# A two-layer latent-attention kernel on one core: a new order for the first tile of the first cross-attention, and a values product in halves in the second

## Chip, core and metric

The kernel runs on one core of a Trainium2 chip. The time is the device time of one execution in microseconds (us); the time of a version is the median over several runs. The engines are TensorE (PE), with its weight loads shown apart as PEld, VectorE (DVE), ScalarE (ACT), GpSimd (POOL) and SyncE (SP, which issues the DMAs). Each has its own instruction stream and works it off in order; they meet in semaphores.

## What is computed

`x` is 16 × 64 × 256 in float32, the context 16 × 256 × 256. Six stages follow one another, each as a residual on a layer norm of `x`:

```python
x = x + L0_xattn(layernorm(x), ctx)      # 16 heads of 64, own layer norms of both, scores clipped to +-11
x = x + L0_attn(layernorm(x))            # latent attention with rotary part, causal
x = x + L0_ffn(layernorm(x))             # attention, then 8 experts, top 2
x = x + L1_xattn(layernorm(x), ctx)      # 16 heads of 16, key padding mask
x = x + L1_attn(layernorm(x))            # causal
x = x + L1_ffn(layernorm(x))             # three layers of +-1 weights
```

The first cross-attention is, cut to what matters here:

```python
lat = layernorm(latents, ln_l_w, ln_l_b); ctx = layernorm(context, ln_c_w, ln_c_b)
q = lat @ Wq; k, v = split(ctx @ Wkv)
attn = softmax(clip(q k^T / 8, -11, 11)); out = (attn v) @ Wo + bo
```

The second has the same form with a bias on q, k, v and a mask on the keys, and no norm of the context.

## The kernel before

The 1024 rows of `x` are T = 8 tiles of 128 rows, each with two batches of 64 latents, and with 512 rows of context. A tile passes a stage at a time. The order on every engine is written out by hand: for each engine there is a function that emits its instructions (`pe_x0`, `act_x0`, `dve_x0`, `pool_x0` for the first cross-attention, `pe_x1`, `act_x1`, `dve_x1` for the second, `pe_self` and so on for the self-attentions).

PE's results that another engine must copy out go through four PSUM banks in a ring (`Ring`). The lists `FILLS` and `X1_FILLS` tell in which order the banks are filled. Fill number n waits until number n − 4 has been emptied; an engine that reads fill n waits for n + 1 increments of one counter. So the lists must name the fills in the order in which PE makes them. Scores and the attended values of x0 have banks of their own.

First cross-attention (x0). Instead of making k, the kernel folds the K weights into the queries: `fill_K` transposes the K weights (`x0wk`, four fills, once), `fill_q` makes the queries of a tile, `fill_A(t, gr)` multiplies the two (A, split into a high and a low float32r part by `A_upper` on ACT and `A_lower` on DVE), and `scores(t, u)` multiplies the context by A. `fill_cT` and `fill_lat` transpose the normalized context and latents; `fill_v(t, i)` makes v, eight fills a tile, from split context (`cT_hi`, `cT_lo`) and split weights (`wv_hi`, `wv_lo`). DVE's `norm(t, part)` normalizes the context and x in four parts; in the last two x is normalized a second time. `ln_done` counts two steps a tile: context and first norm of x, then the second norm. `self_tables` makes small constant tables for the self-attention, behind tile 1. SP issues the loads in the order ctx tile 0, x, constants, columns, q weights, K weights, v weights, ctx tile 1, and more.

Second cross-attention (x1). For tile t, PE's loop in `tiles` has: `scores(t, b)` for both batches (b = 0, 1), `fill_neg` (the transposed negated row maxima, from DVE's `maximum`), `exponents(t, b)` (scores again, keys on partitions, less the maximum), and for the tile before `fill_pv` (values product, 16 heads × 2 key tiles × 2 batches), `fill_T`, `fill_y`; for the tile after `fill_cT`, `fill_lat`, `fill_k`, `fill_q`, `fill_v`. ACT's `exps` makes the exponentials; DVE's `attend` divides, `residual` adds to x and begins the statistics of the next norm, `combine` adds the experts' rows of a later tile. The last tile is interleaved with the first items of the next self-attention in `pe_self`, `act_self` and `dve_self` (span 1, `lo` is its first item).

Of the kernel before, what the change touches and what calls it, by code (L numbers as in the profile page):

```python
# [54 lines left out]
def build(nc, a, out):  # L55

    with ExitStack() as ctx:
# [290 lines left out]
        for _t in range(T):  # L348
            _order += [("x1", _t + 2)] * (_t + 2 < T) + [("attn", _t - 1)] * (_t > 0)
# [123 lines left out]
        FILLS = [(("x0", 0), k) for k in ("cT0", "cT1", "lat", "q0", "q1") + tuple(f"K{i}" for i in range(4)) + tuple(f"A{g}{par}" for g in range(4) for par in range(2))]  # L473
        for t in range(T):
            nxt = t + 1 < T
            FILLS += [(("x0", t), f"v{i}") for i in range(2 * (t > 0), 4)]
# [9 lines left out]
        for t in range(T - 1):  # L486
            X1_FILLS += [(("x1", t - 1), "pv")] * (t > 0) + [(("x1", t + 1), "cT0"), (("x1", t + 1), "cT1"), (("x1", t), "neg0")]
            X1_FILLS += [(("x1", t - 1), "T")] * (t > 0) + [(("x1", t + 1), "lat"), (("x1", t + 1), "k0"), (("x1", t), "neg1")]
            X1_FILLS += [(("x1", t + 1), "k1"), (("x1", t + 1), "q")] + [(("x1", t - 1), "y")] * (t > 0)
            X1_FILLS += [(("x1", t + 1), "v0"), (("x1", t + 1), "v1")]  # L490
        _lo = 2 * T
        X1_FILLS += [(("x1", T - 2), "pv"), (_lo, "hT"), (("x1", T - 1), "neg0"), (("x1", T - 2), "T"), (_lo, "k"), (_lo, "q"), (("x1", T - 1), "neg1"),
                     (_lo, "v"), (_lo + 1, "hT"), (("x1", T - 2), "y"), (_lo + 1, "k"), (_lo + 1, "q"), (("x1", T - 1), "pv"), (("x1", T - 1), "T"),
                     (_lo + 1, "v"), (("x1", T - 1), "y"), (_lo + 2, "hT")]
# [45 lines left out]
        def pe_x0(pe):  # L540
            g = X0

            def fill_cT(t, i):
                if i == 0:
                    pe.wait_ge(ln_done, 2 * t + 2)
# [6 lines left out]
            def fill_lat(t):  # L552
                wait_bank(pe, t, "lat")
# [117 lines left out]
            fill_cT(0, 1)  # L671
            fill_lat(0)
            fill_q(0, 0)
            fill_q(0, 1)
            for i in range(4):
                fill_K(i)
            for gr in range(4):
                fill_A(0, gr)
            for t in range(T):
                nxt = t + 1 < T  # L680
                for i in range(4):
                    if t == 0 or i > 1:
                        fill_v(t, i)
                    scores(t, i)
# [24 lines left out]
        def act_x0(act):  # L709
# [39 lines left out]

            cT(0)  # L750
            lat(0)
            q(0)
            K(0)
            K(2)
            act.wait_ge(ld["x0v"], 16)
# [2028 lines left out]
```

## Time and profile before

| | |
|---|---|
| runs | 1099.9, 1100.84, 1100.64 us; median 1100.64 |
| profiled execution | 1104.84 us, its span 1103.1 us |
| PE busy | 1029.7 us, 93% of the span |
| DVE busy | 640.0 us, 58% |
| ACT busy | 472.2 us, 43% |
| POOL busy | 241.0 us, 22% |
| mean granted PE clock | 0.964 of 2.4 GHz |

All times in rows are from the one profiled execution, from the start of its span. A row of the timeline gives start, duration, engine, line, operation, `out<-in`, and in brackets the idle time before and what ended it. float32 matmuls count as two instructions there. The granted clock is 1.00 or 0.50 of 2.4 GHz; before its first record, near 25 us, the view shows 1.00 whatever it was. The x0 stage lasts from 0 to about 350 us, the x1 tiles from about 764 to 934 us.

### The profile page before, as it was taken

To read this page: it belongs to the slowest core of one execution; us is meant where nothing else is said; L and a number is where in the kernel's file an instruction comes from. 1 tells how busy PE (TensorE), PEld (TensorE's weight loads), DVE (VectorE), ACT (ScalarE), POOL (GpSimd) and SP (SyncE) were. 2 spreads that over 40 slices of the span, in tenths; PEclk is the share of its full clock that TensorE was granted. 3 is DMA by queue.
4 is the path that set the end of the run, shared out by engine and by line. 5 is a ranking of instruction groups with operands and counts; after the bars stand their busy time and mean duration, and the time that the engine had idled before them with its cause. 6 is when DMAs were issued, how large, how long until landed. Compare 5 with 4: busy or idle time off the path is not lost.

```text
span 1103.1 us, 27519 instructions
## 1 busy us (share of the span) xinstructions
PE 1029.7 (93%) x11715; PEld 886.3 (80%) x11715; DVE 640.0 (58%) x1376; ACT 472.2 (43%) x865; POOL 241.0 (22%) x381
## 2 busy tenths in 40 slices
PE   3899999999999899999579999997999999999998
PEld 3788888888887777887479999995787878787887
DVE  3754554544332545775749999975666654345242
ACT  1433333333333566643146767751434433455331
POOL 2212212212111123442404344324200100011000
PEclk9999999999999899998679999997999998999999
DMA  9200000000000800220136557713101000100000
GB/s 311 98 20 20 1 21 20 1 1 1 1 1 1 305 31 3 78 97 13 44 82 221 200 192 268 239 38 105 39 23 40 3 2 19 52 2 2 1 20 19
DMA packets 55672, 72.79 MB, mean 66 GB/s; under 512 B 8504, under 2 KB 48896, under 8 KB 54912
## 3 DMA queue, kind: packets, MB, share of 16 engines
q1 hardware_dynamic: 54016, 66.85, 18.1%
q0 software_dynamic: 1536, 4.20, 1.2%
q8 instruction: 93, 1.52, 0.5%
q14 instruction: 27, 0.22, 0.1%
HBM read 60.02 MB, written 11.01 MB: 64 GB/s over the span
## 4 chain that ended last, share of the span: by engine, by line
PE 83%; DVE 8%; ACT 3%; issue 3%; POOL 1%; DMA 1%; another core or an unknown queue 0%; SPq 0%; DVEq 0%; ACTq 0%; POOLq 0%
PE ps L615 8%; PE ps L630 8%; PE ps L2143 7%; PE ps L2159 6%; PE ps L2499 5%; PE ps L1443 4%; PE ps L599 3%; PE ps L647 3%; PE ps L1094 3%; PE ps L569 3%; PE ps L667 3%; PE ps L1361 3%; PE ps L1400 2%; PE ps L1460 2%; PE ps L1030 2%
## 5 line engine op out<-in xcount | busy, mean ns | idle before, releaser
L371 POOL TENSOR_TENSOR rn_tmp<-rn_cur,eps 128x1 f32<-128x1 f32 x48 | 13.8, 288 | 436.0 <-DVE rn_cur L365 435.9
L744 ACT ACTIVATE x0pT<-ps 128x512 f32<-128x512 f32 x64 | 38.3, 599 | 125.3 <-PE ps L630 125.3
L2295 DVE CAST eh_hi<-eh 128x512 fp32r<-128x512 f32 x60 | 65.6, 1093 | 13.9 <-ACT eh L2205 13.9
L2143 PE MATMUL ps<-moe_xT_hi,ew_1hi 128*128 128x256 f32 x240 | 69.7, 291 | 2.3 <-DVE moe_xT_lo L2289 2.3
L2159 PE MATMUL ps<-ew_2hi,eh_hi 128*128 128x256 f32 x240 | 69.3, 289 | 2.5 <-DVE eh_lo L2297 2.5
L2143 PE MATMUL ps<-moe_xT_lo,ew_1hi 128*128 128x256 f32 x240 | 68.7, 286 | 0.0
L2143 PE MATMUL ps<-moe_xT_hi,ew_1lo 128*128 128x256 f32 x240 | 68.7, 286 | 0.0
L2159 PE MATMUL ps<-ew_2hi,eh_lo 128*128 128x256 f32 x240 | 67.1, 279 | 0.0
L2159 PE MATMUL ps<-ew_2lo,eh_hi 128*128 128x256 f32 x240 | 66.9, 279 | 0.0
L842 DVE TENSOR_TENSOR x0A_lo<-ps,x0A_hi 128x512 fp32r<-128x512 f32 x64 | 41.2, 686 | 33.8 <-ACT x0A_hi L735 33.6
L2499 PE MATMUL ps<-f,ffw 128*128 128x512 f32 x256 | 59.2, 391 | 0.2 <-DVE f L2472 0.2
L2499 PEld LDWEIGHTS ps<-f,ffw 128*128 128x128 f32 x256 | 47.8, 188 | 10.7 <-DVE f L2472 0.8
L926 POOL TENSOR_SCALAR x0pT<-x0pT 128x512 f32<-128x512 f32 x64 | 39.3, 614 | 76.9 <-ACT x0pT L744 74.0
L1443 PEld LDWEIGHTS ps<-sa_v,sa_pT 64*64 64x64 f32 x1536 | 50.0, 138 | 7.3 <-issue 2.9
L1443 PE MATMUL ps<-sa_v,sa_pT 64*64 64x18 f32 x1536 | 54.6, 211 | 0.4 <-issue 0.4
L615 PE MATMUL ps<-x0wv_hi,x0cT_hi 128*128 128x512 f32 x128 | 53.4, 417 | 0.0
L630 PE MATMUL ps<-x0A_hi,x0cT_hi 128*128 128x512 f32 x128 | 52.5, 410 | 0.0
L848 DVE COPY x0v<-ps 128x512 f32<-128x512 f32 x32 | 22.0, 688 | 52.3 <-PE ps L615 52.3
L735 ACT ACTIVATE x0A_hi<-ps 128x512 fp32r<-128x512 f32 x64 | 34.8, 596 | 40.9 <-PE ps L599 40.9
L615 PE MATMUL ps<-x0wv_hi,x0cT_lo 128*128 128x512 f32 x128 | 50.8, 397 | 0.0
L615 PE MATMUL ps<-x0wv_lo,x0cT_hi 128*128 128x512 f32 x128 | 50.8, 397 | 0.0
L2087 POOL TENSOR_TENSOR ew_1lo<-ew,ew_1hi 128x1024 fp32r<-128x1024 f32 x15 | 37.2, 2479 | 61.9 <-ACT ew_1hi L2077 61.9
(329 smaller groups left out, 2834.5 us busy)
## 6 DMA issues: line engine op xcount, KB each, us to landing
ew<-L_ffn_W_dram SPq DMA_DIRECT2D x30, 1024.0 KB, 7.2
x0cin<-ctx_dram SPq DMA_DIRECT2D x8, 512.0 KB, 4.0
x1cin<-ctx_dram SPq DMA_DIRECT2D x8, 512.0 KB, 3.9
xg<-moe_in SPq DMA_DIRECT2D x15, 256.0 KB, 7.9
moe_out<-moe_y SPq DMA_DIRECT2D x15, 256.0 KB, 7.7
moe_in<-padneg SPq DMA_DIRECT2D x3, 1024.0 KB, 12.7
maskrow<-mask_BxS_ik_dram SPq DMA_DIRECT2D x2, 1024.0 KB, 7.5
x0wq<-L_xattn_Wq_dram SPq DMA_DIRECT2D x1, 1024.0 KB, 7.2
```

The source lines that it names most:

```text
L615: last = nc.tensor.matmul(dst, m[:, k, tok * P:tok * P + P], w[:, k, half * 512:half * 512 + 512], start=(k == 0 and n == 0), stop=(k == K ...
L630: last = nc.tensor.matmul(ps[:, S_BANK[u % 2], :], w[:, k, keys], m[:, k, b, pg, :, :, :].rearrange("p a j n -> p (a j n)"), start=(k == 0 ...
L735: nc.scalar.activation(g.A_hi[:, kc, :, pg, par, :, :].rearrange("p b j n -> p j b n"), bank_of(t, f"A{gr}{par}").rearrange("p (j b n) -> ...
L744: nc.scalar.activation(g.pT[:, u, :], ps[:, S_BANK[u % 2], :], ACT.Exp, scale=64.0 ** -0.5).then_inc(C0.exp, 1)
L842: nc.vector.tensor_tensor(g.A_lo[:, kc, :, pg, par, :, :].rearrange("p b j n -> p j b n"), bank_of(t, f"A{gr}{par}").rearrange("p (j b n) ...
L926: nc.gpsimd.tensor_scalar(g.pT[:, u, :], g.pT[:, u, :], high, low, ALU.min, ALU.max).then_inc(C0.clip, 1)
L1443: last = nc.tensor.matmul(RS.bank(n, "pv")[rows_b, hd * XVW:hd * XVW + XVW], g.pT[rows_b, r, at_p:at_p + N], g.v[n % 3][rows_b, hd, :], st ...
L2087: nc.gpsimd.tensor_tensor(lo, w, hi.bitcast(F32), ALU.subtract).then_inc(MO.w_lo_pool, 1)
L2143: last = nc.tensor.matmul(ps[:, n % 3, j * BT:j * BT + BT], w[b % 2][:, i, f * P:f * P + P], v[b % 2][:, i, :], start=(i == 0 and m == 0), ...
L2159: last = nc.tensor.matmul(ps[:, O_BANK[b % 2] + c, 0:D], v[n % 3][:, j * BT + c * P:j * BT + c * P + P], w[b % 2][:, f, :], start=(f == 0 ...
L2295: nc.vector.tensor_copy(eh_hi[n % 3][:, :], eh[n % 3][:, :]).then_inc(MO.hi, 1)
L2499: last = nc.tensor.matmul(ps[:, 2 + f % 4, :], w[:, k, f * P:f * P + P], src[part][:, k, :], start=(k == 0 and part == 0), stop=(k == ks - ...
```

## The change

Start of x0:

- DVE no longer begins with the six instructions that make `identb`, `causalb`, `row_is`, `one_row` and `pick_row`; they stand at the head of `self_tables`. It begins `norm(0, 0)` when the context tile is there, waits for x ahead of `norm(0, 1)` and for the constants ahead of `norm(0, 3)`.
- `fill_cT(t, 0)` waits for `ln_done` of 2t + 1; `fill_lat(t)` has the wait for 2t + 2.
- K0 and K1 are transposed ahead of the latents, K2 and K3 ahead of q; v0 is made ahead of A0, v1 between A1 and A2. SP issues the K weights ahead of the q weights.
- ACT runs a one-column Exp first, and makes both parts of `wv_hi` ahead of q. On DVE the split of the context is a function of its own, `cT_split`, for tile 0 behind K3, followed by both parts of `wv_lo`.

Second cross-attention:

- `fill_pv(t, half)` makes eight heads; in the loop the transposes of the next context stand between the halves. `fill_y` stands ahead of the second `fill_neg` instead of ahead of the second `exponents`.
- DVE has `attend` behind `cT_lower`, and `residual` ahead of `combine`, `k` and `q`. The numbers of the row statistics (`X1_ROWS`) are exchanged to match.
- The last tile, in `pe_self`, `act_self` and `dve_self`, is interleaved anew in the same sense.

```diff
-            _order += [("x1", _t + 2)] * (_t + 2 < T) + [("attn", _t - 1)] * (_t > 0)
+            _order += [("attn", _t - 1)] * (_t > 0) + [("x1", _t + 2)] * (_t + 2 < T)
...
-        FILLS = [(("x0", 0), k) for k in ("cT0", "cT1", "lat", "q0", "q1") + tuple(f"K{i}" for i in range(4)) + tuple(f"A{g}{par}" for g in range(4) for par in range(2))]
+        FILLS = [(("x0", 0), k) for k in ("cT0", "cT1", "K0", "K1", "lat", "K2", "K3", "q0", "q1", "v0", "A00", "A01", "A10", "A11", "v1", "A20", "A21", "A30", "A31")]
...
             def fill_cT(t, i):
                 if i == 0:
-                    pe.wait_ge(ln_done, 2 * t + 2)
+                    pe.wait_ge(ln_done, 2 * t + 1)
...
             def fill_lat(t):
+                pe.wait_ge(ln_done, 2 * t + 2)
...
             dve.sem_inc(rn_rstd, 2)
-            for part in range(4):
-                norm(0, part)
-            nc.vector.memset(g.v[:, :, :, 64:VW], 1.0).then_inc(C0.ones, 1)
+            norm(0, 0)
+            dve.wait_ge(ld["x"], 16)
+            norm(0, 1)
+            norm(0, 2)
+            dve.wait_ge(ld["const"], 32)
+            norm(0, 3)
             cT(0)
-            q(0)
             K(1)
             K(3)
...
+            cT_split(0)
+            nc.vector.memset(g.v[:, :, :, 64:VW], 1.0).then_inc(C0.ones, 1)
+            for i in range(KD):
+                dve.wait_ge(C0.w_hi, i + 1)
...
+            q(0)
+            A_lower(0, 0)
+            A_lower(0, 1)
+            v(0, 1)
+            A_lower(0, 2)
+            A_lower(0, 3)
             for part in range(4):
                 norm(1, part)
...
                     if old:
-                        fill_pv(t - 1)
+                        fill_pv(t - 1, 0)
                     fill_cT(t + 1, 0)
                     fill_cT(t + 1, 1)
+                    if old:
+                        fill_pv(t - 1, 1)
                     scores(t, 1)
                     fill_neg(t, 0)
                     if old:
                         fill_T(t - 1)
                     fill_lat(t + 1)
                     fill_k(t + 1, 0)
+                    if old:
+                        fill_y(t - 1)
                     fill_neg(t, 1)
                     exponents(t, 0)
                     fill_k(t + 1, 1)
                     fill_q(t + 1)
-                    if old:
-                        fill_y(t - 1)
                     exponents(t, 1)
...
                     maximum(t, 0)
-                    if t > 0:
-                        attend(t - 1)
                     norm(t + 1)
                     cT_lower(t + 1, 0)
                     cT_lower(t + 1, 1)
+                    if t > 0:
+                        attend(t - 1)
                     maximum(t, 1)
+                    if t > 0:
+                        residual(t - 1)
                     if t + 2 < T:
                         combine(t + 2)
                     k(t + 1)
                     q(t + 1)
-                    if t > 0:
-                        residual(t - 1)
...
                 t = T - 1
+                fill_hT(lo)
                 x1_scores(t, 0)
-                x1_pv(t - 1)
-                fill_hT(lo)
+                x1_pv(t - 1, 0)
+                fill_qk(lo, "k")
+                x1_pv(t - 1, 1)
                 x1_scores(t, 1)
                 x1_neg(t, 0)
                 x1_T(t - 1)
-                fill_qk(lo, "k")
                 fill_qk(lo, "q")
+                x1_y(t - 1)
                 x1_neg(t, 1)
                 x1_exponents(t, 0)
                 fill_v(lo)
                 fill_hT(lo + 1)
-                x1_y(t - 1)
+                fill_qk(lo + 1, "k")
                 x1_exponents(t, 1)
-                fill_qk(lo + 1, "k")
                 fill_qk(lo + 1, "q")
-                x1_pv(t)
+                x1_pv(t, 0)
+                fill_v(lo + 1)
+                x1_pv(t, 1)
                 scores(lo)
                 x1_T(t)
-                fill_v(lo + 1)
                 x1_y(t)
...
+            whole(X0.wk[:, :, :], weight("L0_xattn_Wkv")[:, :, 0:INNER], ld["x0k"])
             whole(X0.wq[:, :, :], weight("L0_xattn_Wq"), ld["x0q"])
-            whole(X0.wk[:, :, :], weight("L0_xattn_Wkv")[:, :, 0:INNER], ld["x0k"])
```

PE at the very start, before. L549 are the transposes of the context, L556 of the latents, L569 q, L581 the K weights (the number of matmuls is that of the program here, half of the trace's for float32 products):

```order
L549 MATMUL ps<-cst,x0cn 128x128 [waits ln_done,ld_const]
L549 MATMUL ps<-cst,x0cn 128x128 x7
L556 MATMUL ps<-cst,x0lat 128x128 x2
L569 MATMUL ps<-x0latT,x0wq 128x128 [waits sa_by_act,ld_x0q]
L569 MATMUL ps<-x0latT,x0wq 128x128 x7
L569 MATMUL ps<-x0latT,x0wq 128x128 [waits sa_by_act]
L569 MATMUL ps<-x0latT,x0wq 128x128 x7
L581 MATMUL ps<-cst,x0wk 128x128 [waits sa_by_dve,ld_x0k]
```

and now, at the same place, up to the first product of v (L615):

```order
L548 MATMUL ps<-cst,x0cn 128x128 [waits ln_done,ld_const]
L548 MATMUL ps<-cst,x0cn 128x128 x7
L581 MATMUL ps<-cst,x0wk 128x128 [waits ld_x0k]
L581 MATMUL ps<-cst,x0wk 128x128 x7
L556 MATMUL ps<-cst,x0lat 128x128 [waits sa_by_act,ln_done]
L556 MATMUL ps<-cst,x0lat 128x128
L581 MATMUL ps<-cst,x0wk 128x128 [waits sa_by_dve]
L581 MATMUL ps<-cst,x0wk 128x128 x3
L581 MATMUL ps<-cst,x0wk 128x128 [waits sa_by_act]
L581 MATMUL ps<-cst,x0wk 128x128 x3
L569 MATMUL ps<-x0latT,x0wq 128x128 [waits sa_by_dve,sa_by_act,ld_x0q]
```

The K weights' transposes moved ahead of the latents' and of q, and the wait for the second norm moved from the first to the fifth row.

PE in a tile of the second cross-attention, before: first scores (L1054, L1057), values product (L1094), second scores:

```order
L1054 MATMUL ps<-padneg,one_row 128x256 x4
L1057 MATMUL ps<-x1kT_218,x1qbd_216 128x256 x4
L1094 MATMUL ps<-x1v_219,x1pT 64x18 x64
L991 MATMUL ps<-cst,x1cin 128x128 x8
L1054 MATMUL ps<-padneg,one_row 128x256 x4
L1057 MATMUL ps<-x1kT_218,x1qbd_216 128x256 x4
```

and now, with the context's transposes (L1013) between two halves (L1117), ahead of the second scores instead of behind the whole product:

```order
L1076 MATMUL ps<-padneg,one_row 128x256 x4
L1079 MATMUL ps<-x1kT_218,x1qbd_216 128x256 x4
L1117 MATMUL ps<-x1v_219,x1pT 64x18 x32
L1013 MATMUL ps<-cst,x1cin 128x128 x8
L1117 MATMUL ps<-x1v_219,x1pT 64x18 x32
L1076 MATMUL ps<-padneg,one_row 128x256 x4
L1079 MATMUL ps<-x1kT_218,x1qbd_216 128x256 x4
```

Further down in the same tile, the y product (L1134) now stands between the last row of k0 (L1042) and the second negated maximum (L1086):

```order
L1042 MATMUL ps<-x1cT_hi,x1w_lo 128x512
L1134 MATMUL ps<-xw,x1attT 128x256 x2
L1086 MATMUL ps<-identb,x1neg_223 128x128
L1097 MATMUL ps<-x1negT_224,pick_row 128x128 x4
L1100 MATMUL ps<-x1qbd_216,x1kT_218 128x128 x4
```

Before, it stood behind q (L1006), ahead of the second exponents (L1075, L1078):

```order
L1020 MATMUL ps<-x1cT_hi,x1w_lo 128x512
L1006 MATMUL ps<-x1latT,xw 128x128 x4
L1110 MATMUL ps<-xw,x1attT 128x256 x2
L1075 MATMUL ps<-x1negT_225,pick_row 128x128 x4
L1078 MATMUL ps<-x1qbd_216,x1kT_218 128x128 x4
```

So y moved up past the second negated maximum, the first exponents, k1 and q.

## Rows read from the trace of the kernel before

**Rows 1.** The page: shares of the chain that ended last, by engine

```profile
PE 83%; DVE 8%; ACT 3%; issue 3%; POOL 1%; DMA 1%; another core or an unknown queue 0%; SPq 0%; DVEq 0%; ACTq 0%; POOLq 0%
```

**Rows 2.** Timeline of the start: start, duration, engine, line, operation, count, idle before

```profile
0.80 0.45 SPq L2559 DMA_DIRECT2D x0cin<-ctx_dram  x1
...
2.83 0.43 SPq L2553 DMA_DIRECT2D x0wq<-L_xattn_Wq_dram  x1
...
7.02 0.23 DVE L2703 CAST identb<-cst 128x128 bf16<-128x128 f32 x1 [7.02 <-DMA col<-cols_dram]
...
8.04 1.07 DVE L291 BATCH_NORM_STATS2 ln_st<-x0cin 128x6 f32<-128x256 f32 x3
...
13.31 0.41 DVE L314 TENSOR_SCALAR x0lat<-x_res,ln_mv,ln_rs 128x256 f32<-128x256 f32 x1
...
15.56 0.41 DVE L314 TENSOR_SCALAR x0lat<-x0lat,ln_mv,ln_rs 128x256 f32<-128x256 f32 x1 [0.93 <-POOL ln_rs L309]
...
16.12 1.94 PE L549 MATMUL ps<-cst,x0cn 128*128 128x128 f32 x8 [16.12 <-DVE x0lat L314]
...
17.29 1.28 ACT L714 ACT_TABLE_LOAD   x1 [17.29 <-PE ps L549]
...
20.21 6.05 PE L569 MATMUL ps<-x0latT,x0wq 128*128 128x128 f32 x32 [1.72 <-ACT x0latT L719]
...
32.12 1.23 DVE L884 TENSOR_TENSOR x0wv_lo<-x0wv,x0wv_hi 128x1024 fp32r<-128x1024 f32 x1
...
38.19 1.07 DVE L291 BATCH_NORM_STATS2 ln_st<-x0cin 128x6 f32<-128x256 f32 x3
...
45.95 0.52 DVE L314 TENSOR_SCALAR x0lat<-x0lat,ln_mv,ln_rs 128x256 f32<-128x256 f32 x1 [0.93 <-POOL ln_rs L309]
```

**Rows 3.** DMA issues of the start: size, median us from issue to landing

```profile
x0cin<-ctx_dram SPq DMA_DIRECT2D x1, 512.0 KB, 4.0
...
x0wq<-L_xattn_Wq_dram SPq DMA_DIRECT2D x1, 1024.0 KB, 7.2
```

**Rows 4.** PE by stretch: length, busy, instructions, granted clock, DMA share, GB/s

```profile
35.00:38.50 3.50, 3.45 (x21) 0.52 0.02 5
```

**Rows 5.** Chain that ended last, tile 0: `fill_v(0, 4)`

```profile
49.89 1.39 PE ps L615 x6
```

**Rows 6.** Waits from 775 to 930 us: total, times, longest

```profile
PE ps L1064 <- DVE x1neg L1244: 5.9, 7, 0.9
```

**Rows 7.** Timeline of one tile of the second cross-attention, on PE, DVE, ACT

```profile
823.83 3.91 PE L1094 MATMUL ps<-x1v,x1pT 128*64 128x18 f32 x128
...
832.95 0.23 PE L1064 MATMUL ps<-identb,x1neg 128*128 128x128 bf16 x1 [0.91 <-DVE x1neg L1244]
...
837.14 1.37 DVE L1223 TENSOR_SCALAR x1qbd<-ps,col,cst 128x128 f32<-128x128 f32 x4
...
834.69 2.12 ACT L1176 ACTIVATE x1pT<-ps,maskT 128x1024 f32<-128x1024 f32 x2 [1.20 <-PE ps L1078]
```

**Rows 8.** Chain that ended last: first scores of three tiles, and a y product

```profile
822.70 0.22 PE ps L1054 x4
...
837.10 0.86 PE ps L1110 x4
...
842.48 0.22 PE ps L1054 x4
...
863.72 0.22 PE ps L1054 x4
```

**Rows 9.** PE by stretch, behind two values products; columns as in rows 4

```profile
847.40:850.80 3.40, 3.40 (x33) 0.52 0.08 20
...
926.00:932.80 6.80, 6.80 (x75) 0.50 0.00 0
```

**Rows 10.** Timeline of DVE: first copy of v in a later tile of x0

```profile
88.18 0.69 DVE L848 COPY x0v<-ps 128x512 f32<-128x512 f32 x1 [4.08 <-PE ps L615]
```

**Rows 11.** Timeline of ACT: `attT` of the last tile

```profile
931.07 0.62 ACT L1182 ACTIVATE x1attT<-ps,col 128x128 f32<-128x128 f32 x2 [7.40 <-PE ps L1103]
```

More of the change, by code:

```diff
@@ L671, in pe_x0 @@
             fill_cT(0, 1)
+            fill_K(0)
+            fill_K(1)
             fill_lat(0)
+            fill_K(2)
+            fill_K(3)
             fill_q(0, 0)
             fill_q(0, 1)
[L675 to L678, printed above, removed]
+            fill_v(0, 0)
+            fill_A(0, 0)
+            fill_A(0, 1)
+            fill_v(0, 1)
+            fill_A(0, 2)
+            fill_A(0, 3)
             for t in range(T):
@@ L748, in attT @@
                 nc.scalar.activation(g.attT[:, 0:4, :], bank_of(t, "T0"), ACT.Copy).then_inc(C0.by_act, 1)
+            nc.scalar.activation(exp_next[:, :], cst[:, 0:1], ACT.Exp)
             cT(0)
+            K(0)
             lat(0)
-            q(0)
-            K(0)
             K(2)
             act.wait_ge(ld["x0v"], 16)
+            for i in range(KD):
+                nc.scalar.activation(g.wv_hi[:, i, :], g.wv[:, i, :], ACT.Copy).then_inc(C0.w_hi, 1)
+            q(0)
+            v(0, 0)
             for gr in range(4):
                 A_upper(0, gr)
-                if gr < KD:
-                    nc.scalar.activation(g.wv_hi[:, gr, :], g.wv[:, gr, :], ACT.Copy).then_inc(C0.w_hi, 1)
             for t in range(T):
                 nxt = t + 1 < T
-                if t == 0:
-                    v(t, 0)
                 exp(t, 0)
@@ L788, in self_tables @@
         def self_tables(dve):
+            nc.vector.tensor_copy(identb[:, :], ident).then_inc(setup, 1)
+            nc.vector.tensor_copy(causalb[:, :], cst[:, C_CAUSAL:C_CAUSAL + N]).then_inc(setup, 1)
+            nc.vector.tensor_reduce(row_is[:, :], ident.rearrange("p (r c) -> p c r", c=32)[:, 0:8, :], AX_X, ALU.add).then_inc(setup, 1)
+            dve.wait_ge(setup, 3)
+            nc.vector.tensor_copy(one_row[:, :], row_is[:, 0:1].broadcast_to((P, P)))
+            for i in range(2):
+                nc.vector.tensor_tensor(pick_row[:, i, :], row_is[:, i:i + 1].broadcast_to((P, P)), row_is[:, 2 + i:3 + i].broadcast_to((P, P)), ALU.add)
             route_start(dve)
@@ L896, in dve_x0 @@
                     cT(t + 1)
+                    cT_split(t + 1)
                 if more:
@@ L1081, in exponents, with fill_pv @@
                 last.then_inc(C1.e_ps, 1)
-            def fill_pv(t):
-                pe.wait_ge(C1.exp, 4 * t + 4)
-                if t == 0:
-                    pe.wait_ge(C1.ones, 1)
-                R1.wait_emptied(pe, t, "v0")
-                R1.wait_emptied(pe, t, "v1")
-                R1.wait_free(pe, t, "pv")
-                for hd in range(H):
+            def fill_pv(t, half):
+                if half == 0:
+                    pe.wait_ge(C1.exp, 4 * t + 4)
+                    if t == 0:
+                        pe.wait_ge(C1.ones, 1)
+                    R1.wait_emptied(pe, t, "v0")
+                    R1.wait_emptied(pe, t, "v1")
+                    R1.wait_free(pe, t, "pv")
+                for hd in range(8 * half, 8 * half + 8):
                     hf, r, par = hd // 8, hd // 2 % 4, hd % 2
@@ L1096, in fill_pv @@
                                                     start=(kt == 0), stop=(kt == 1), skip_group_check=True)
-                last.then_inc(C1.fill, 1)
+                if half == 1:
+                    last.then_inc(C1.fill, 1)
             def fill_T(t):
@@ L1823, in dve_self @@
                 x1_maximum(t, 0)
+                k(lo)
                 x1_attend(t - 1)
```

41 lines of the change are left out of this document (13 added, 28 removed).

## The prediction

> **What bounds the kernel now.** I read the chain of work that ended last first: TensorE (PE) holds 83% of it [rows 1]. A change pays only where PE waits, or where it runs at the lower of its clocks; on VectorE (DVE), ScalarE (ACT) or GpSimd a shorter list is worth nothing by itself. Then I went to the two places that the diff touches and read them in order of time.
>
> The start. PE does nothing until 16.12 us [rows 2]. Context tile 0 is issued at 0.80 and lands 4.0 us later [rows 2, 3], at 4.8, but DVE begins its statistics at 8.04, behind the constants' load and six small table instructions. The normalized context is there at 13.31 + 0.41 = 13.72, but the transposes wait for the second normalization of x too, which ends at 15.56 + 0.41 = 15.97. Then q, K, A and v follow, with PE idle in pieces; the last part runs at a granted clock of 0.52, which is 1.2 GHz for nearly all of it [rows 4]. The first marker after which nothing is changed is `fill_v(0, 4)`, at 49.89 [rows 5].
>
> The second cross-attention. In the steady loop PE waits once a tile, for the second negated maximum: seven waits, 5.9 us, at most 0.9 [rows 6]; the one at 832.95 ended 0.91 us of idling [rows 7]. The tile is otherwise full. Its start-to-start time is 842.48 − 822.70 = 19.78 us, and 863.72 − 842.48 = 21.24 for the tile in which the granted clock fell to 0.52 (1.2 GHz), right behind the values product [rows 8, 9]. PE had been busy with 128 short matmuls for 3.91 us before that [rows 7]. Such a stretch stands behind three of the seven products in the trace; that of the last tile fills 926.0 to 932.8 [rows 9].
>
> **The start, step by step.** Instructions are the same ones; the sum is a new schedule of them.
> 1. Statistics at 4.9 instead of 8.04: 3.1 us. The landing of x and the 5-column GpSimd step are not later than that by more than the 0.1 us that I allow.
> 2. `fill_cT` waits for the context alone: 15.97 − 13.72 = 2.25 us. First transposes at 16.12 − 3.1 − 2.3 = 10.7.
> 3. The K weights now come ahead of the q weights in SP's queue, so they land where those did, at 2.83 + 7.2 = 10.0 [rows 2, 3], before K0 is reached at 12.7; the q weights land in the other's place, before 15. No wait.
> 4. PE then goes through 8 context transposes (1.94 us at the clock of the start [rows 2]), 8 for K (as much), 2 for x, 8 for K: to 17.0. The q products take their 6.05 us again or, were the clock up by then, some 3.6: done at 20.6 to 23.1.
> 5. DVE finishes K3 at 17.7, splits the context (0.69 + 1.23), and makes the low part of the v weights, 2 × 1.23 [rows 2]: 22.1 with the memset. `fill_v(0, 0)` starts at about 22.1.
> 6. v0 (1.4 us), A0, A1 (1.1 each), v1, A2, A3: here PE waits only where DVE's lower halves free a bank, about 0.3 us. Scores begin at 29.7, with v1 done. Before they began behind v0 alone, with v1 still to do.
> 7. What is late next is DVE's normalization of tile 1. It starts behind the last A at 31.6 and takes what it took, 45.95 + 0.52 − 38.19 = 8.3 us [rows 2]. PE gets to `fill_lat(1)` at 39.0 and waits until 39.9; then the bank of v3 is freed by DVE only at 41.6, behind `norm(2, 0)`. So `fill_v(0, 4)` starts at 41.7 instead of 49.89: **8.2 us gained**. Without those two late steps it would be 10.6. With q at the slow end and v0, v1 at 1.2 GHz (1.2 us more each) it would be 4.9.
>
> The table load on ACT (1.28 us at 17.29 [rows 2]) is moved ahead of the context and disappears behind the loads. The Trainium skill, ScalarE: Activation LUTs (What ACT_TABLE_LOAD costs), gives about 2.66 us for a switch with its drain; the trace shows 1.28, then 0.02 us to the next activation. By either price the load is hidden in the new order, and its gain is inside the 8.2.
>
> The six table instructions cost DVE 1.0 us (7.02 to 8.04 [rows 2]) behind tile 1. Before the next tile's first copy of v DVE had waited 4.08 us for PE [rows 10], so nothing is lost; without that cover it would be 1.0.
>
> **The second cross-attention, step by step.** The values product becomes 2 × 64 matmuls, at 3.91 / 128 = 30 ns each as before, so the halves cost nothing themselves; the context's transposes stand between them. `attend` is moved behind `cT_lower` on DVE, and the product ends where transposes ended, so the attended values are there 0.5 us before `fill_T` asks for them.
> The gain is `fill_y`, 0.86 us [rows 8], which moves into the 0.91 us wait. It needs only `attT` from ACT, done at about 831.0, before the k product has ended. Six tiles × 0.86 = **5.2 us**. What is late next: `exponents(t, 1)` follows `exponents(t, 0)` now by k1 and q alone: 837.10 less the start of ACT's exponentials, 834.69, is 2.41 us, and ACT needs 2.12 [rows 7, 8]: covered by 0.3 us. DVE puts `residual` (1.9) and `combine` (2.0) ahead of `k` and `q`: q's copies, which ended at 837.14 + 1.37 = 838.5 [rows 7], end at about 839.0, and the next scores start at 841.6. Cover 2.6 us.
> **The clock.** In the trace the low stretches begin at the end of an unbroken values product. With full-size transposes in its middle and no wait in the tile I expect the two in the loop to go: 2 × (21.24 − 19.78) = **2.9 us** (bounds: 0, and as much lost again if they come elsewhere). The Trainium skill, TensorE: Matmul & The Clock Gate (Terms), prices a throttled stretch at half its length: for 3.4 us, 1.7, against 1.46 in the rows; by the page the two would be worth 3.4. The rows decide.
> **The last tile** is reordered more. k and q of the next item used to stand between `exponents(7, 1)` and the product, 2.0 us against ACT's 2.12; now only q does, 1.0, so PE waits 1.1 longer. `fill_y(7)` follows `fill_T(7)` at once, where a v product had covered ACT's 0.62 [rows 11]: 0.7 more. The two together are 1.8, and 1.9 with what PE waits at its start. If the clock stays up, half of the 6.8 us at 1.2 GHz [rows 9] is saved, 3.3 to 3.4. Between 1.9 lost and 1.4 gained; I take **0.2 lost**, since the longer wait ahead of it speaks for the fall.
>
> **Sum.** 8.2 + 5.2 + 2.9 − 0.2 = 16.1. The profiled execution took 1104.84 us, 4.2 over the median of the runs, 1100.64; it would be 1088.7, and the median 1084.5. I say 1085.
>
> **The rivals.**
> (a) The clock keeps its low stretches, or they wander to other tiles, and the last tile runs slow: 8.2 + 5.2 − 1.9 = 11.5, 1089. For it: four of the seven products are not followed by such a stretch with the same code, so it hangs on little. The Trainium skill, the same page (A second HAM failure mode), blames small idle gaps of PE between groups for such swings. By that rule the longer waits of the last tile bring it and the halves do nothing, while the removed wait helps; in the rows PE was busy 3.91 us ahead of the fall.
> (b) The wait is only exchanged: PE now stops at `exponents(t, 1)`, or `fill_y` finds its bank or `attT` late. Then the loop gives nothing and the clock nothing: 8.2 − 0.2, 1092.6. Cover 0.3 us speaks weakly against it; a part of it (0.3 a tile) would make 1087.
> (c) The start gives 4.9 (slow clock through q, v0, v1): 1088.
> (d) Slower: DVE works in order, so `residual` and `combine` ahead of `k` and `q` hold the next `scores(t+1, 0)` if the gathered rows for `combine` or the y product come late. It decides from 2.6 us lateness. To undo all and reach +2 us it takes 18 us over six tiles, 3 a tile beyond the cover: 1103. The rows show `combine` at its place without waiting, so little speaks for it.
> (e) The start gives nothing because DMA, not DVE, is the limit there, and the loop gives (b): no change, 1100. Landing at 4.8 against 8.04 speaks against it.
>
> **Numbers.** Forecast 0.60 (1082 to 1087), (a) 0.20, (b) 0.07, (c) 0.07, (d) 0.03, (e) 0.03. Range 1080.5 to 1091: it takes in (a) and (c) and, below, the start without its two late steps (2.4 more) and the better last tile. A measurement of this kernel tells about 0.2%, 2.2 us, from no change. Faster 0.94, same 0.03, slower 0.03.
>
> **What would show it.** In the changed profile: the first transposes near 10.7; the first scores near 30; `fill_v(0, 4)` near 41.7, with DVE named as the one waited for at `fill_lat(1)` and at v4. In the loop, start-to-start times of 18.9 us, the wait at the second negated maximum gone, no wait at `exponents(t, 1)`, no granted clock of 0.5 behind a product. I am wrong if the wait stands before another instruction with the same length, if tiles still take 19.8, or if the first scores come after 33.

## The result, and the profile after

The changed kernel takes 1092.2 us, median of five runs (1091.04 to 1095.08), against 1100.64 (1099.9 to 1104.45) before: a ratio of 0.9923, with a 95% interval of 0.9899 to 0.9946. That is 8.4 us faster. I had said 16.1 faster, at 1085 and between 1080.5 and 1091. The direction was right, the size not.

The profiled execution took 1091.17 us (before 1104.84). The page, its span, its busy times and the shares of the chain that ended last (to be read beside [rows 1]):

```profile
span 1089.4 us, 27524 instructions
...
PE 1025.6 (94%) x11715; PEld 883.0 (81%) x11715; DVE 640.2 (59%) x1376; ACT 472.3 (43%) x866; POOL 242.8 (22%) x381
...
PE 84%; DVE 7%; ACT 3%; issue 3%; POOL 2%; DMA 1%; DVEq 0%; POOLq 0%; ACTq 0%
```

PE still bounds the kernel. In this pair of profiles the gain is 13.7 us, so I read where it arises by comparing the same instruction in both traces.

The timeline of PE at the start: start, duration, engine, line, operation, count, and in brackets the idle time before and what ended it. It answers to [rows 2] and [rows 5].

```profile
10.75 1.94 PE L548 MATMUL ps<-cst,x0cn 128*128 128x128 f32 x8 [10.75 <-DVE x0lat L314]
...
29.32 0.50 PE L630 MATMUL ps<-x0A_hi,x0cT_hi 128*128 128x512 f32 x1
...
39.58 0.44 PE L556 MATMUL ps<-cst,x0lat 128*128 128x128 f32 x2 [0.79 <-DVE x0lat L314]
...
41.15 0.50 PE L615 MATMUL ps<-x0wv_hi,x0cT_hi 128*128 128x512 f32 x1 [1.13 <-DVE x0v L863]
```

First transposes at 10.75, first scores at 29.32, `fill_v(0, 4)` at 41.15 instead of 49.89: 8.7 us earlier. (49.89 is the start in the chain, where a product begins only when the one before it has ended. The chain has 41.15 here too.) The two waits that come late next are there too, 0.79 at the latents of tile 1 and 1.13 at v4.

The timeline of PE in a tile of the second cross-attention (the same tile as in [rows 7] and [rows 8]):

```profile
827.18 0.29 PE L1076 MATMUL ps<-padneg,one_row 32*128 32x256 bf16 x4
...
828.38 2.05 PE L1117 MATMUL ps<-x1v,x1pT 128*64 128x18 f32 x64
830.35 1.09 PE L1013 MATMUL ps<-cst,x1cin 128*128 128x128 f32 x8
831.38 2.05 PE L1117 MATMUL ps<-x1v,x1pT 128*64 128x18 f32 x64
...
836.46 1.03 PE L1134 MATMUL ps<-xw,x1attT 128*128 128x256 f32 x4
837.45 0.23 PE L1086 MATMUL ps<-identb,x1neg 128*128 128x128 bf16 x1
...
846.04 0.29 PE L1076 MATMUL ps<-padneg,one_row 32*128 32x256 bf16 x4
```

The y product (L1134) ends as the negated maximum (L1086) begins, and no idle time stands in brackets. The tile takes 846.04 − 827.18 = 18.86 us, against 19.78. From 770 to 880 us the trace names no wait of PE, and the granted clock is 1.00 throughout.

The last tile is another matter. PE's waits from 870 to 935 us: who waited for whom, total, times, longest:

```profile
PE ps L1387 <- ACT sa_hT L1646: 1.5, 1, 1.5
PE ps L1356 <- DVE h L393: 1.4, 1, 1.4
PE ps L1117 <- ACT x1pT L1202: 1.2, 1, 1.2
PE ps L1420 <- ACT sa_pT L1684: 0.8, 1, 0.8
PE ps L1134 <- ACT x1attT L1208: 0.7, 1, 0.7
PE ps L1086 <- DVE x1neg L1270: 0.6, 1, 0.6
```

I had foreseen the third and the fifth (1.1 and 0.7). The second stands at the start of the tile, where the old order waits 1.0 already; I had allowed 0.1 more and it is 0.4. The first I had not foreseen. It shows in the timelines of ACT and PE:

```profile
897.72 2.12 ACT L1202 ACTIVATE x1pT<-ps,maskT 128x1024 f32<-128x1024 f32 x2 [1.21 <-PE ps L1100]
899.99 0.39 ACT L1646 ACTIVATE sa_hT<-ps 128x256 f32<-128x256 f32 x1
...
900.44 1.16 PE L1387 MATMUL ps<-sa_hT,w_sq 128*128 128x128 f32 x8 [1.51 <-ACT sa_hT L1646]
...
905.29 2.05 PE L1117 MATMUL ps<-x1v,x1pT 128*64 128x18 f32 x64 [1.16 <-ACT x1pT L1202]
```

The product `k(lo+1)` (L1387) now stands ahead of `exponents(7, 1)`. It needs `hT(lo+1)` copied by ACT, and in ACT's order that copy stands behind the exponentials of 2.12 us. So PE waits 1.51 us and reaches the second exponents later, and ACT its second exponentials.

Behind that, the clock. PE by stretch (length, busy, instructions, granted clock, DMA share, GB/s), to be held against [rows 9]:

```profile
890.00:907.20 17.20, 13.93 (x286) 1.00 0.01 2
907.20:921.00 13.80, 13.09 (x135) 0.51 0.01 2
```

The stretch at 1.2 GHz in the last tile is 13.8 us long; before it was 6.8. It begins as the first half of the last values product ends (905.29 + 2.05 = 907.34), so the halves did not prevent it here. Of the 17.2 us ahead of it PE was busy for 13.93.

To put a price on the last tile I take one length in every trace: from the second scores of tile 6 to the first output product of the self-attention behind (`sa_attT`). In the changed kernel these are:

```profile
871.09 0.29 PE L1076 MATMUL ps<-padneg,one_row 32*128 32x256 bf16 x4
...
936.11 1.13 PE L1486 MATMUL ps<-w_sq,sa_attT 128*128 128x256 f32 x4
```

and in the kernel before:

```profile
890.37 0.40 PE L1054 MATMUL ps<-padneg,one_row 32*128 32x256 bf16 x4
...
949.80 1.13 PE L1460 MATMUL ps<-w_sq,sa_attT 128*128 128x256 f32 x4
```

65.02 us against 59.43: here 5.6 us are given back. The lead of the changed kernel is thus 8.7 us at v4; 783.07 − 770.56 = 12.5 at the first scores of tile 1; 890.37 − 871.09 = 19.3 at the second scores of tile 6; and 949.80 − 936.11 = 13.7 behind the last tile, which is what remains at the end. The 3.8 us between v4 and tile 1 I had not forecast: the trace of before has a stretch of 6.8 us at 1.2 GHz at 366.2, at the end of the first cross-attention, and this one has none there. Other traces of kernels with the new start have it (at 358.7 in `start_only`, 358.0 in `y_late`), so it is not a gain of the change that I could show.

### The profile page after: what moved, and what is told of

It is laid out like the page before. It is cut to its first block, busy times and chain, and to the rows that moved or that the text cites. A ratio compares the mean times of both kernels' runs of the same rounds, so it can differ in the third digit from the quotient of the medians.

```text
span 1089.4 us, 27524 instructions
## 1 busy us (share of the span) xinstructions
PE 1025.6 (94%) x11715; PEld 883.0 (81%) x11715; DVE 640.2 (59%) x1376; ACT 472.3 (43%) x866; POOL 242.8 (22%) x381
## 4 chain that ended last, share of the span: by engine, by line
PE 84%; DVE 7%; ACT 3%; issue 3%; POOL 2%; DMA 1%; DVEq 0%; POOLq 0%; ACTq 0%
PE ps L615 8%; PE ps L630 8%; PE ps L2171 7%; PE ps L2187 7%; PE ps L2527 5%; PE ps L1469 4%; PE ps L599 3%; PE ps L1117 3%; PE ps L647 3%; PE ps L1387 3%; PE ps L667 3%; PE ps L569 3%; PE ps L1486 2%; PE ps L1426 2%; PE ps L1052 2%
## 5 line engine op out<-in xcount | busy, mean ns | idle before, releaser
L2323 DVE CAST eh_hi<-eh 128x512 fp32r<-128x512 f32 x60 | 63.4, 1056 | 13.9 <-ACT eh L2233 13.9
L2527 PEld LDWEIGHTS ps<-f,ffw 128*128 128x128 f32 x256 | 47.8, 188 | 10.7 <-DVE f L2500 0.8
L615 PE MATMUL ps<-x0wv_hi,x0cT_hi 128*128 128x512 f32 x128 | 53.0, 414 | 3.1 <-issue 1.5
L2325 DVE TENSOR_TENSOR eh_lo<-eh,eh_hi 128x512 fp32r<-128x512 f32 x60 | 49.8, 831 | 2.1
L615 PE MATMUL ps<-x0wv_hi,x0cT_lo 128*128 128x512 f32 x128 | 50.6, 395 | 0.0
## 6 DMA issues: line engine op xcount, KB each, us to landing
moe_in<-padneg SPq DMA_DIRECT2D x3, 1024.0 KB, 13.2
```

The lines of the kernel that those rows point to most:

```text
L615: last = nc.tensor.matmul(dst, m[:, k, tok * P:tok * P + P], w[:, k, half * 512:half * 512 + 512], start=(k == 0 and n == 0), stop=(k == K ...
L2323: nc.vector.tensor_copy(eh_hi[n % 3][:, :], eh[n % 3][:, :]).then_inc(MO.hi, 1)
L2325: nc.vector.tensor_tensor(eh_lo[n % 3][:, :], eh[n % 3][:, :], eh_hi[n % 3][:, :].bitcast(F32), ALU.subtract).then_inc(MO.split, 1)
L2527: last = nc.tensor.matmul(ps[:, 2 + f % 4, :], w[:, k, f * P:f * P + P], src[part][:, k, :], start=(k == 0 and part == 0), stop=(k == ks - ...
```

## The experiments

Each kernel was timed beside the kernel before on the same chip, and the ratio is to that. "Last tile" below is the length defined above, from the one profile of each kernel.

**One part at a time.** First the new start alone: the second cross-attention is put back as before (the diff is against the changed kernel).

```diff
-            def fill_pv(t, half):
+            def fill_pv(t):
...
-                        fill_pv(t - 1, 0)
+                        fill_pv(t - 1)
```

> The new start of the first cross-attention alone, with the second cross-attention as before. Theory (the parts add up; the start is worth what its profile shows): 8.5 us faster, ratio 0.992, fill_v(0, 4) near 41.2 us as in the changed kernel. Rival (the start's gain is partly given back in the stages behind it, for instance by the clock): under 6 us faster.

1092.8 us against 1104.02, ratio 0.9907 (0.9886 to 0.9929), so 10.3 us by ratio, 7.8 to 12.6. In its trace v4 starts at 40.08, and low stretches stand behind the products at 816.1, 857.1 and 915.1: the start carries its gain alone and does nothing for the clock of the loop. The 8.5 us expected lie in the interval.

Then the new loop alone, with start and last tile as before (the diff is against the kernel before).

```diff
-                        fill_pv(t - 1)
+                        fill_pv(t - 1, 0)
                     fill_cT(t + 1, 0)
                     fill_cT(t + 1, 1)
+                    if old:
+                        fill_pv(t - 1, 1)
...
+                    if old:
+                        fill_y(t - 1)
                     fill_neg(t, 1)
```

> The new steady loop of the second cross-attention alone, with start and last tile as before. Theory (what is gained is the removed wait, 0.92 us in six tiles; the low clock behind the products in the profile of before was no regular cost): 5.5 us faster, start-to-start 18.9 us. Rival (the halves keep the clock up and that saves 2.9 more against typical runs): 8.5 us faster.

1093.92 against 1104.02, ratio 0.9917 (0.9887 to 0.9946): 9.2 us, 6.0 to 12.5. No low stretch in the loop, one of 6.8 us in the last tile, at 921.1; the tile is 944.96 − 887.12 = 57.84 us long. The time agrees with the rival (8.5 us, the halves save clock too) better than with the 5.5 us that I had expected, which lie just outside.

Then the new last tile alone (against the kernel before).

```diff
-                x1_scores(t, 0)
-                x1_pv(t - 1)
                 fill_hT(lo)
+                x1_scores(t, 0)
+                x1_pv(t - 1, 0)
+                fill_qk(lo, "k")
+                x1_pv(t - 1, 1)
...
+                x1_pv(t, 0)
+                fill_v(lo + 1)
+                x1_pv(t, 1)
```

> The new last tile alone, with start and loop as before. Theory (its new waits cost, and with them the longer stretch at 1.2 GHz): 4 to 6 us slower. Rival (my prediction: 0.2 us lost, within 1.4 gained and 1.9 lost).

1106.71 against 1104.02, ratio 1.0024 (1.0004 to 1.0043): 2.6 us slower. It has the same four waits, 1.5, 1.4, 1.2 and 0.7 us, and in this profile no low stretch in the last tile:

```profile
889.79 0.29 PE L1054 MATMUL ps<-padneg,one_row 32*128 32x256 bf16 x4
...
950.09 0.70 PE L1462 MATMUL ps<-w_sq,sa_attT 128*128 128x256 f32 x2
```

That is 60.30 us, against 59.43 in the kernel before, whose last tile has the low stretch. So the waits alone do not always bring the clock down. I had expected 4 to 6 us slower; by the interval (0.4 to 4.7) only the lower end of that is left.

The three parts alone add up to 10.3 + 9.2 − 2.6 = 16.9 us, which is near the 16.1 of my sum (term by term less so: 10.3 for 8.2, 9.2 for 8.1, 2.6 lost for 0.2), but the whole change gives 8.4 (13.2 in the second comparison, below). The next run shows where the parts do not add up.

**The changed kernel with the old last tile**: the whole change but for `pe_self`, `act_self` and `dve_self` (against the changed kernel).

```diff
-                fill_hT(lo)
                 x1_scores(t, 0)
                 x1_pv(t - 1, 0)
-                fill_qk(lo, "k")
                 x1_pv(t - 1, 1)
+                fill_hT(lo)
...
                 x1_exponents(t, 1)
+                fill_qk(lo + 1, "k")
                 fill_qk(lo + 1, "q")
                 x1_pv(t, 0)
-                fill_v(lo + 1)
                 x1_pv(t, 1)
```

> The changed kernel with the last tile as before. Theory (the new last tile costs 4 to 6 us): 4 to 6 us faster than the changed kernel, some 14 us faster than the kernel before, about 1086.5. Rival (the last tile is neutral; the loop or the start gave less than their profile shows): 8.4 us faster than before, as the changed kernel is.

1083.51 us (1082.6 to 1085.0) against 1104.02, ratio 0.9828 (0.9807 to 0.9849). That is 19.0 us faster, and start and loop alone gave 10.3 + 9.2 = 19.5: these two add up. The new last tile is what does not. It costs 2.6 us alone, and behind the new start and loop 10.5 or 5.7 us, by 0.9923 and 0.988 (below) against 0.9828. I had expected 14 us faster than before. In the profile the last tile is shorter by 10.1 us than in the changed kernel, 928.42 − 873.49 = 54.93:

```profile
873.49 0.29 PE L1076 MATMUL ps<-padneg,one_row 32*128 32x256 bf16 x4
...
928.42 1.13 PE L1486 MATMUL ps<-w_sq,sa_attT 128*128 128x256 f32 x4
```

Its waits from 870 to 935 us, and PE by stretch:

```profile
PE ps L1076 <- DVE sa_neg L1834: 1.0, 1, 1.0
PE ps L1420 <- ACT sa_pT L1684: 0.8, 1, 0.8
PE ps L1086 <- DVE x1neg L1270: 0.7, 1, 0.7
PE ps L1117 <- ACT x1pT L1202: 0.3, 1, 0.3
PE ps L1097 <- ACT x1pT L1202: 0.2, 1, 0.2
```

```profile
905.00:921.00 16.00, 15.24 (x302) 1.00 0.38 109
```

The waits sum to 3.0 us, those of the changed kernel to 6.2: 3.2 us of the 10.1. The low stretch accounts for most of the rest: by my estimate, half of its 13.09 us of busy time, 6.5 us. Some 0.4 stay without a name. One part of the change is thus a loss, and the kernel without it beats both.

**The changed kernel again**, beside the next ones on one chip; nothing is edited.

> The changed kernel once more, beside the two below, for a second profile of it. Theory (the last tile's waits fall again, 1.4 + 1.5 + 1.2 + 0.7 us, and behind them a stretch at 1.2 GHz of 10 us or more): the same four waits, a low stretch behind the last product, ratio near 0.992. Rival (the 13.7 us stretch was one execution's accident): the same waits, a stretch of 7 us or none, ratio near 0.987.

1091.84 against 1102.83, ratio 0.988 (0.9852 to 0.9908). The same four waits, the same low stretch (13.7 us at 909.0), a last tile of 65.07 us, as the theory had it; the ratio is nearer to the rival's. The gain is 13.2 us by this ratio and 11.0 by the medians. Two of the six runs took 1086.96 and 1087.04 us at a mean granted clock of 0.970 and 0.971, the other four 1090.95 to 1093.15 at 0.964 to 0.968. So the clock does not fall as much in every execution; where it held in those two no trace shows. In the first comparison the kernel before had come out at 1100.64, and in the three comparisons since at 1104.02, 1102.83 and 1103.85, of 17, 11 and 20 runs.

**One row of the last tile.** In the changed kernel only `k(lo+1)` goes back behind the second exponents.

```diff
-                fill_qk(lo + 1, "k")
                 x1_exponents(t, 1)
+                fill_qk(lo + 1, "k")
                 fill_qk(lo + 1, "q")
```

> The changed kernel with one row moved: the k product of the item after the next stands behind the last exponents again, as in the kernel before. Theory (that row makes two of the four new waits: 1.5 us for hT ahead of it, and 1.2 us ahead of the last values product, which it used to cover): both gone but some 0.2 us each, 2.4 us faster than the changed kernel, and more where the clock then holds. Rival (the waits are only moved behind it): within 0.5 us of the changed kernel.

1085.28 (1083.46 to 1086.4), ratio 0.9831 (0.9806 to 0.9856), 6.6 us less than the changed kernel beside it by the medians, 5.4 by the ratios (expected: 2.4, and more where the clock holds). Waits from 870 to 935 us, and PE by stretch:

```profile
PE ps L1356 <- DVE h L393: 1.4, 1, 1.4
PE ps L1097 <- ACT x1pT L1202: 1.1, 1, 1.1
PE ps L1420 <- ACT sa_pT L1684: 0.8, 1, 0.8
PE ps L1134 <- ACT x1attT L1208: 0.7, 1, 0.7
PE ps L1086 <- DVE x1neg L1270: 0.6, 1, 0.6
PE ps L1117 <- ACT x1pT L1202: 0.3, 1, 0.3
```

```profile
890.00:905.00 15.00, 13.35 (x271) 1.00 0.01 2
905.00:921.00 16.00, 15.03 (x278) 1.00 0.20 58
```

The wait of 1.5 is gone, the one ahead of the values product is 0.3 instead of 1.2, and a wait of 1.1 stands at the second exponents: 1.3 us less in all. And the granted clock stays at 1.00. The last tile takes 931.30 − 873.58 = 57.72 us, 7.3 less than in the changed kernel. Most of the cost of that one row in the profile is the clock.

**And the first wait.** On top of that, `hT(lo)` goes back behind the first scores.

```diff
-                fill_hT(lo)
                 x1_scores(t, 0)
+                fill_hT(lo)
                 x1_pv(t - 1, 0)
```

> The kernel with the k product put back, and hT of the first item behind the first scores of the last tile instead of ahead of them. Theory (hT ahead of the scores costs PE 1.4 us where it had waited 1.0 anyway, so 0.4 to 0.5 us; the last products keep their high clock): 0.5 us faster than 1085.3, ratio near 0.983. Rival (any shift there brings the low stretch back): 4 us or more slower.

1083.66 (1083.07 to 1085.75) against 1103.85, ratio 0.9824 (0.98 to 0.9847): last tile 57.28 us. Its waits are those of the kernel above, but for the 1.4 that became 1.0, as in the old order. The interval holds the value of the kernel above as well, so the 0.5 us that I had expected is neither shown nor refuted.

**The halves.** The changed kernel with the old last tile, and the product of the loop undivided again. DVE's `attend` goes back ahead of the norm with it, which the lines below do not show.

```diff
                         fill_pv(t - 1, 0)
+                        fill_pv(t - 1, 1)
                     fill_cT(t + 1, 0)
                     fill_cT(t + 1, 1)
-                    if old:
-                        fill_pv(t - 1, 1)
```

> Old last tile, new start, new loop, but the loop's values product undivided ahead of the context's transposes, with attend where it stood; y stays at its new place. Theory (the halves keep the clock up, two or three low stretches of 3.4 us come back, 1.46 us each): 3 to 4.5 us slower than with halves (1083.5), so near 1087.5, tiles of 18.9 us where the clock holds. Rival (the removed wait alone keeps the clock up): no low stretch behind a product, 1083.5 within 1.

1090.51 (1088.02 to 1091.81) against 1102.83, ratio 0.9888 (0.9863 to 0.9913): about 6.6 us more than with the halves (0.9888 against 0.9828; by the two intervals about 3 to 10), where I had expected 3 to 4.5. From 770 to 885 us its trace has no wait of PE at all, and yet PE by stretch reads:

```profile
834.50:837.90 3.40, 3.40 (x34) 0.50 0.11 16
855.00:858.40 3.40, 3.40 (x28) 0.50 0.02 5
875.50:878.90 3.40, 3.40 (x32) 0.50 0.00 0
```

Three stretches, each behind an undivided product, in tiles that never wait. First scores two tiles apart, from its timeline of PE:

```profile
829.54 0.29 PE L1076 MATMUL ps<-padneg,one_row 32*128 32x256 bf16 x4
...
870.26 0.29 PE L1076 MATMUL ps<-padneg,one_row 32*128 32x256 bf16 x4
```

(870.26 − 829.54) / 2 = 20.36 us a tile, against 18.90 without a stretch: 1.46 each, as in the kernel before. Three make 4.4 of the 6.6 us.

The other traces bear it out. In the six profiles of kernels whose loop has the undivided product (before, `start_only`, `tail_only`, `stats_first`, `order_only` and this one) a low stretch follows 16 of the 36 products of the loop, two or three in each; in the eight with the halves none of 48. That `attend` moves with the halves is a rival for the 6.6 us that no run separates. It does not explain the clock by way of a wait, since PE waits nowhere in this loop.

**The y product.** The changed kernel with the old last tile and the halves, but `fill_y` and `residual` at their old places.

```diff
-                    if old:
-                        fill_y(t - 1)
                     fill_neg(t, 1)
...
                     fill_q(t + 1)
+                    if old:
+                        fill_y(t - 1)
                     exponents(t, 1)
```

> Old last tile, new start, halves, but y and the residual at their old places in the loop. Theory (the move of y is worth the removed wait and nothing else): the wait at the second negated maximum is back, 0.9 us in six tiles, 5.5 us slower than 1083.5, near 1089, no low stretch behind a product. Rival (the wait is what lets the clock fall): low stretches in two or three tiles too, near 1093.

1091.55 (1089.33 to 1093.2), ratio 0.9889 (0.9865 to 0.9913), so by the ratios 6.7 us worse than with the move (expected: 5.5). The wait is back, from 770 to 885 us:

```profile
PE ps L1086 <- DVE x1neg L1270: 5.0, 6, 0.8
```

The clock stays up in the loop, so the halves do that without the moved y. In this profile the last tile, whose order is the old one, has a stretch of 6.8 us.

**The start, divided.** Statistics at once and the split waits for the context, without the new order of fills (against the kernel before, as the next one).

```diff
-            for part in range(4):
-                norm(0, part)
+            norm(0, 0)
+            dve.wait_ge(ld["x"], 16)
+            norm(0, 1)
+            norm(0, 2)
+            dve.wait_ge(ld["const"], 32)
+            norm(0, 3)
```

> The kernel before with one part of the new start: DVE begins the statistics when the context is there (the tables behind tile 1), and the context's transposes no longer wait for the second norm of x. The order of the fills is as before. Theory (the end of the first norms is what PE waits for, and the rest of the start is moved by as much as the second norm of x is): transposes at 10.7, v4 near 45, 5 us faster. Rival (the order behind it takes it back): under 3 us faster.

And the new order of fills, with the table instructions first and the old wait ahead of the transposes.

```diff
+            fill_K(0)
+            fill_K(1)
...
+            fill_K(2)
+            fill_K(3)
...
-            for i in range(4):
-                fill_K(i)
-            for gr in range(4):
-                fill_A(0, gr)
+            fill_v(0, 0)
+            fill_A(0, 0)
+            fill_A(0, 1)
+            fill_v(0, 1)
+            fill_A(0, 2)
+            fill_A(0, 3)
```

> The other part of the new start alone: K ahead of the latents, v0 and v1 between the A fills, the K weights first, the table load and the weights' split early; but the tables and both norms first, as before, and the transposes behind them. Theory (the parts add up to 8.7 us in the profile): transposes at 16.1, v4 3.5 to 4.5 us ahead of before's 49.9, as much faster. Rival (the order pays only with the early statistics): under 1.5 us faster.

The first: 1099.29 against 1103.85, ratio 0.9965 (0.9944 to 0.9987), transposes at 10.81, v4 at 44.11 (here and next as in the chain). The second: 1099.7, ratio 0.9968 (0.995 to 0.9986), transposes at 15.96, v4 at 45.85, with a new wait of 1.97 us:

```profile
44.28 1.09 PE L549 MATMUL ps<-cst,x0cn 128*128 128x128 f32 x8 [1.97 <-DVE x0lat L314]
```

So v4 is 5.8 and 4.0 us earlier than in [rows 5], together more than the 8.7 of the whole start. Of the order alone, as of the whole, the trace shows PE waiting for DVE's normalization of tile 1 at the end; of the statistics alone it does not. By the ratios they are worth 3.9 and 3.5 us (intervals 1.4 to 6.2 and 1.5 to 5.5), together less than the 10.3 of the whole start, though the intervals allow as much. This stays open. The forecasts were 5 us for the first and 3.5 to 4.5 for the second.

**The start's two late waits.** Old last tile, and half of tile 1's normalization done ahead of A's lower halves, v3 ahead of `norm(2, 0)`.

```diff
+            norm(1, 0)
+            norm(1, 1)
...
-            for part in range(4):
-                norm(1, part)
+            norm(1, 2)
+            norm(1, 3)
```

> The kernel with old last tile, new start and new loop (1083.5 us), and on DVE the statistics of tile 1 set into the wait for the first A, and the copy of v3 of tile 0 ahead of the next statistics. Theory (the two late steps of the new start, 0.8 us at the latents' transposes and 1.1 at v4, are DVE's order and nothing else): both waits gone, v4 near 39.2, 1.9 us faster, near 1081.6. Rival (a later A_lower or cT holds PE instead): within 0.5 of 1083.5.

1083.87 (1081.6 to 1087.6) against 1103.85, ratio 0.9814 (0.979 to 0.9839). In the trace both waits are gone, and v4 starts 2.6 us earlier than in the kernel it is built on (40.77; by the chain 38.38, 2.4 us):

```profile
38.00 0.38 PE L556 MATMUL ps<-cst,x0lat 128*128 128x128 f32 x2
38.13 0.48 PE L615 MATMUL ps<-x0wv_hi,x0cT_hi 128*128 128x512 f32 x1
```

The gain (1081.6 expected) does not stand out of the medians: 1083.87 against 1083.51 of the kernel it is built on, 0.9814 against 0.9828. The profiled execution was the longest, 1087.6, and in it the clock fell in the last tile although its order is the old one:

```profile
892.20:895.60 3.40, 3.40 (x31) 0.50 0.00 0
909.20:916.00 6.80, 6.80 (x56) 0.50 0.01 2
```

## Why the prediction was half right

**The start: right.** Transposes at 10.7 forecast, 10.75 found; first scores 29.7 and 29.32; v4 41.7 and 41.15; 8.2 us and 8.7. Both late waits stood where they were named, and taking them away made v4 2.4 to 2.6 us earlier (2.4 forecast). Alone the start is worth 10.3 us (7.8 to 12.6) by the ratio.

**The y product in the wait: right.** The wait went, the tile takes 18.86 us, and no new wait appeared at `exponents(t, 1)`; with y at its old place the wait is back, 5.0 us in six tiles. Rival (b) falls with that. The times differ by 6.7 us, of which 5.0 are this wait; its profile also has the low stretch in the last tile.

**The clock of the loop: right in mechanism, too small in size.** Without the halves three stretches came back, in a loop without waits; with them there was none in eight profiles of kernels that had halves in the loop. I had taken 2.9 us from the two stretches of one trace; the halves are worth about 6.6 us (3 to 10), of which 4.4 are seen. One reading was off: the trace of before has eight values products and not seven (six in the loop, two in the last tile), so five and not four are without a stretch behind them. The rule that I weighed in rival (a), from the Trainium skill, TensorE: Matmul & The Clock Gate (A second HAM failure mode), put the swings down to small idle gaps; by it the halves would do nothing. In the loop the measurement decides against it as the only cause, with three stretches in tiles where PE never waited.

**The last tile: this step failed.** The term was 0.2 us lost, taken between 1.9 lost and 1.4 gained. Against the kernel with the new loop and the old last tile, which has a low stretch of 6.8 us there as the kernel before had, it cost 65.02 − 57.84 = 7.2 us. Two things were wrong in it. I counted PE's rows between the exponents and the product, but not what the row that moved up must itself wait for: ACT's copy of `hT(lo+1)`, queued behind 2.12 us of exponentials. The waits grew by 3.2 us, 1.5 of it this one, where I had 1.9 as the worst. And I bounded the clock by a stretch that either stays at 6.8 us or goes; it doubled, to 13.8, another 3.5 us by half its growth of 7.0. The waits that I had named are about right in size; the unnamed one of 1.5 us and the clock make the miss. Here rival (a) came nearer: the low stretch was there in both profiles that have the longer waits behind the new loop, and with the wait of 1.5 us taken out the clock stayed up. That agrees with the page just named, for this place, though a cause it is not yet shown to be. Its conditions are not settled: the new last tile alone had all the waits and no low stretch in its profile (and cost 2.6 us, not 6 to 10), and the old one had low stretches in six profiles of nine, three of them among the five behind the new loop or a part of it. Which wait matters most is open too, since moving the one row changed three at once.

**From the profile to the median: the second step that failed.** I subtracted the 4.2 us by which the profiled execution lay over the median of three runs, without a run that showed that the changed kernel's would lie so too. For the changed kernel the profile lay 1.0 us under the median. Of the distance between the 1084.5 of the sum and 1092.2, 5.2 us are this step, and only 2.5 are in the sum itself (1088.7 against 1091.17), where the 7.0 too little for the last tile were partly made up by the 3.8 us at 366. Later medians of the kernel before, 1102.83 to 1104.02, show that 1104.84 was an ordinary execution. The first comparison gives 0.9923 and the second 0.988; their intervals meet only at 0.990 to 0.991, so I would call the change 8 to 13 us faster.

Rivals (c) and (e) fall with the start: v4 came 8.7 us earlier. (d) falls with the loop: DVE's longer list ahead of `k` and `q` held nothing up.

## What to carry to other kernels

When a row moves ahead of another engine's long instruction, look up on that engine what its own operands stand behind; the 1.5 us wait here was visible in ACT's order. Price a new wait not at its length alone: here a wait of 1.5 us, with the two that moved along with it, went together with about 6 us of clock. Try cutting such products with full-size work, and time each place both alone and on top of the others, since the last tile cost 2.6 us alone and 6 to 10 behind the rest. And do not subtract the distance of one profile from the median of three runs.

## What the runs showed of the hardware

The undivided product, 64 float32 matmuls of 18 columns (128 instructions in the trace) with PE busy throughout, was followed by 3.4 us at 1.2 GHz in three tiles that had no wait at all. With eight full-size transposes (1.09 us) in its middle there was no such stretch in the loop, in 48 products; without them there was one behind 16 of 36. The last values product of the changed kernel, divided too but by a v product, has a stretch of 13.7 us in both profiles, behind 1.2 and 1.5 us waits. A stretch of 3.4 us cost 1.46 us (in `tail_only` and `start_only` 1.4: tiles of 21.2 us against 19.8). The Trainium skill, TensorE: Matmul & The Clock Gate (Terms), prices it at half its length, which makes 1.7 as an estimate; the rows decide. Within one kernel the time of a run follows its mean granted clock. Of the 20 runs of the kernel before on one chip, those at 0.966 took 1100.46 to 1101.17 us, and the two at 0.958 and 0.955 took 1108.92 and 1109.17.
